# One spectral transform for keys and values and one for the weights, with partition blocks exchanged by DMA

## The reference, cut to what matters

```python
def _layernorm(x, axis=-1, eps=1e-05):
    return (x - mean) / sqrt(var + eps)

# Q = layernorm(x), K = V = ctx; B, L, D = 16, 64, 512; H = 8, topk = int(2 * log(64)) = 8
qf = jnp.fft.fft(q, axis=2)
kf = jnp.fft.fft(k, axis=2)
corr = jnp.fft.ifft(qf * jnp.conj(kf), axis=2).real
w, idx = jax.lax.top_k(corr.transpose(0, 1, 3, 2), topk)
w = jax.nn.softmax(w, axis=-1)
for i in range(topk):
    g = jnp.minimum(idx[:, :, None, :, i] + pos, L - 1)
    out = out + w[:, :, None, :, i] * jnp.take_along_axis(v, g, axis=2)
# then
x = x + tanh(g_xattn[0]) * attention
gate, up = layernorm(x) @ W_gate.T, layernorm(x) @ W_up.T      # 512 -> 1792
x = x + tanh(g_ffn[0]) * ((silu(gate) * up) @ W_down.T)
```

## Time and profile before

| | us |
|---|---|
| median of 3 runs | 226.29 (226.14 to 226.38) |
| the profiled execution, its own time | 226.31 |
| its span in the trace | 224.5 |
| PE busy, of the span | 215.6 (96%) |
| DVE busy | 149.8 (67%) |
| POOL busy | 134.2 (60%) |
| ACT busy | 98.4 (44%) |
| DMA: bytes, mean rate | 16.68 MB, 74 GB/s |

### The profile page before, as it was taken

How to read it: one execution, slowest core, us unless ns; L and a number is a source line. 1 busy time by engine, 2 the same in 40 slices (tenths; PEclk the granted TensorE clock), 3 DMA queues, 4 the chain that set the end, 5 groups by cost and what they waited for, 6 DMA issues and landing times.

```text
span 224.5 us, 6750 instructions
## 1 busy us (share of the span) xinstructions
PE 215.6 (96%) x2787; PEld 149.6 (67%) x2787; DVE 149.8 (67%) x424; ACT 98.4 (44%) x191; POOL 134.2 (60%) x148
## 2 busy tenths in 40 slices
PE   7899699799999999999999999999999999999994
PEld 2543278575395856788468965776689477967961
DVE  2799997998799777598739495576765516413321
ACT  2574146666466542744544543544414422410320
POOL 1325637989888888659774877449656292530240
PEclk9999979999999999999999999999999999999999
DMA  6899942004201122202121402202031100211001
GB/s 172 279 449 427 386 164 50 0 4 50 47 4 41 33 9 64 50 3 25 26 47 26 121 0 26 70 3 51 0 96 23 26 0 3 70 26 50 0 3 47
DMA packets 19885, 16.68 MB, mean 74 GB/s; under 512 B 15888, under 2 KB 16272, under 8 KB 19472
## 3 DMA queue, kind: packets, MB, share of 16 engines
q1 hardware_dynamic: 19856, 16.26, 25.0%
HBM read 10.49 MB, written 2.10 MB: 56 GB/s over the span
## 4 chain that ended last, share of the span: by engine, by line
PE 89%; DVE 4%; DMA 2%; POOL 1%; issue 1%; SPq 1%; ACT 0%; DVEq 0%
PE psum L825 46%; PE psum L990 22%; PE psum L808 11%; PE psum L941 4%; DMA x_sb<-x 2%; PE psum L838 1%; DVE xn L769 1%; POOL prod_lo L512 1%; DVE prod L675 1%; PE psum L877 1%; PE psum L908 1%; PE psum L889 1%; PE psum L926 1%; DVE raw_stats L644 1%; PE psum L891 1%
## 5 line engine op out<-in xcount | busy, mean ns | idle before, releaser
L825 PE MATMUL psum<-xt_hi,wg 128*128 128x128 f16 (+1 forms) x504 | 54.9, 215 | 0.0
L825 PE MATMUL psum<-xt_lo,wg 128*128 128x128 f16 (+1 forms) x504 | 54.8, 215 | 0.0
L825 PE MATMUL psum<-xt_hi,wu 128*128 128x128 f16 (+1 forms) x504 | 54.0, 213 | 0.0
L825 PE MATMUL psum<-xt_lo,wu 128*128 128x128 f16 (+1 forms) x504 | 53.9, 213 | 0.0
L825 PEld LDWEIGHTS psum<-xt_hi,wg 128*128 128x128 f16 x504 | 45.8, 99 | 5.8 <-issue 3.8
L550 POOL TENSOR_TENSOR hid_lo<-hid,hid_hi 128x512 f16<-128x512 f32 (+2 forms) x32 | 33.5, 1051 | 26.7 <-ACT hid_hi L635 26.6
L825 PEld LDWEIGHTS psum<-xt_hi,wu 128*128 128x128 f16 x504 | 44.7, 98 | 5.2 <-issue 4.7
L825 PEld LDWEIGHTS psum<-xt_lo,wg 128*128 128x128 f16 x504 | 46.1, 99 | 0.6
L825 PEld LDWEIGHTS psum<-xt_lo,wu 128*128 128x128 f16 x504 | 45.0, 98 | 0.5
L990 PE MATMUL psum<-wd,hid_hi 128*128 128x512 f16 x112 | 42.5, 379 | 0.0
L990 PE MATMUL psum<-wd,hid_lo 128*128 128x512 f16 x112 | 42.4, 379 | 0.0
(11 more groups left out here) (83 smaller groups left out, 340.3 us busy)
## 6 DMA issues: line engine op xcount, KB each, us to landing
out<-x_sb SPq DMA_DIRECT2D x8, 256.0 KB, 2.3
wg<-w_gate SPq DMA_DIRECT2D x1, 1792.0 KB, 11.2
wu<-w_up SPq DMA_DIRECT2D x1, 1792.0 KB, 14.9
wd<-w_down SPq DMA_DIRECT2D x1, 1792.0 KB, 19.0
ctx_sb<-ctx SPq DMA_DIRECT2D x1, 1024.0 KB, 21.0
x_sb<-x SPq DMA_DIRECT2D x1, 1024.0 KB, 22.8
x_sb<-x SPq DMA_DIRECT2D x2, 256.0 KB, 3.9
ctx_sb<-ctx SPq DMA_DIRECT2D x2, 256.0 KB, 4.4
```

The costliest lines, as they stand in the source:

```text
L825: last = nc.tensor.matmul(psum[:, bank, a * n:(a + 1) * n], w[:, k, m * P:(m + 1) * P], xt[:, e, k, tok], start=(k == 0 and part == 0), st ...
```

## The change

Keys and values are the same tensor, so from pair 1 on `kspec` now makes one transform of 128 different outputs: 64 of the even spectrum and 64 of the odd one (matrix "values"). `vspec` is left for pair 0 alone. `wspec` makes one transform with the 64 even and 64 odd outputs of the weights (matrix "weights") instead of two. The turned forms are no longer outputs of a matmul. Instead, ScalarE copies the two banks into `v_spec` (`vcopy`, 128 x 1024) and partitions 0 to 63 of them into `k_spec` (`kcopy`, 64 x 1024), and a new step `turn`, issued by SyncE, moves blocks of 32 partitions by DMA: `turn:p` fills the other half of `k_spec` from `v_spec` (two transfers of 32 rows of 4 KB, semaphore `k_moved`), `turn:p.1` fills `v_turned` (one of 31 rows, three of 32 rows, and the last rows of ctx from memory, semaphore `v_moved`). `prod` waits for `k_moved`, the last two `mix_prod` for `v_moved`. `mixed` has one buffer instead of two.

Both normalisations (`q_norm`, `xn`) move from VectorE to ScalarE as `Identity` with a scale and a bias per row; GpSimd makes the bias with one more operation on a column after each 1/sqrt. The loads of pair 3 move behind the second weight tensor. The warm-up groups go from 12, 4 and 9 matmuls to 12, 1 and 10. `ORDER` is a new list.

```diff
-FORWARD = ("even_kv", "even", "odd_v", "odd")
+FORWARD32 = ("even_kv", "even", "odd_v", "odd")
+FORWARD = ("query", "values", "weights")
...
+    even = np.hstack([cos(f), nyquist, -sin(f[1:])])
+    odd = np.hstack([cos(g), -sin(g)])
+    odd_v = odd.copy()
+    odd_v[-1] -= odd_v.sum(0)
...
+    return np.hstack([even, even]), np.hstack([even, odd_v]), np.hstack([even, odd]), lags, mix_plain, mix_turned
...
-        return min(p, 2) if p < 4 else 3
+        return min(p, 4)
...
-            load(ctx_sb, cv, 2, 4, ctx_loaded[2])
-            load(x_sb, xv, 2, 4, x_loaded[2])
+            load(ctx_sb, cv, 2, 3, ctx_loaded[2])
+            load(x_sb, xv, 2, 3, x_loaded[2])
             sp.dma_start(wg[:, :, :], w_gate).then_inc(gate_loaded, 16)
             sp.dma_start(wu[:, :, :], w_up).then_inc(up_loaded, 16)
+            load(ctx_sb, cv, 3, 4, ctx_loaded[3])
+            load(x_sb, xv, 3, 4, x_loaded[3])
             sp.dma_start(wd[:, :, :], w_down).then_inc(down_loaded, 16)
-            load(ctx_sb, cv, 4, PAIRS, ctx_loaded[3])
-            load(x_sb, xv, 4, PAIRS, x_loaded[3])
+            load(ctx_sb, cv, 4, PAIRS, ctx_loaded[4])
+            load(x_sb, xv, 4, PAIRS, x_loaded[4])
             for step, p, n in order:
                 e = p % 2
+                if step == "turn":
+
+                    if n == 0:
+                        sp.wait_ge(v_copied, copies(p))
+                        if p == 2:
+                            sp.wait_ge(mixed_done, 4)
+                        if p >= 2:
+                            sp.wait_ge(prod_done, 2 * p - 2)
+                        for to, first in ((64, 32), (96, 0)):
+                            sp.dma_start(k_spec[to:to + 32, e, :, :], v_spec[first:first + 32, e, :, :])\
+                              .then_inc(k_moved[e], 16)
+                    else:
+                        if p > 2:
+                            sp.wait_ge(mixed_done, 4 * p - 4)
+                        for to, first, count in ((1, 33, 31), (32, 0, 32), (64, 96, 32), (96, 64, 32)):
+                            sp.dma_start(v_turned[to:to + count, e, :, :], v_spec[first:first + count, e, :, :])\
+                              .then_inc(v_moved[e], 16)
+                        sp.dma_start(v_turned[0:1, e, :, :], last_rows[p:p + 1, :, :]).then_inc(v_moved[e], 16)
...
+                nc.gpsimd.tensor_scalar(shift[tok, n:n + 1], mean, rstd[tok, n:n + 1], -1.0, ALU.mult,
+                                        ALU.mult).then_inc(shift_done, 1)
...
+            def normalise(to, p, tok, n, normed_done):
+                nc.scalar.activation(to, x_sb[tok, p, :], ACT.Identity, bias=shift[tok, n:n + 1],
+                                     scale=rstd[tok, n:n + 1]).then_inc(normed_done, 1)
...
+                if step == "vcopy" and p > 0:
                     act.wait_ge(k_spectra, p + 1)
...
+                    nc.scalar.activation(v_spec[:, e, :, :], psum[:, k_bank(p, 0):k_bank(p, 1) + 1, :], ACT.Copy,
+                                         scale=SPEC).then_inc(v_copied, 1)
...
+                    nc.scalar.activation(k_spec[0:L, e, :, :], psum[0:L, k_bank(p, 0):k_bank(p, 1) + 1, :], ACT.Copy,
                                          scale=SPEC).then_inc(k_copied, 1)
...
                 if step == "prod":
                     dve.wait_ge(q_spectra, p + 1)
-                    dve.wait_ge(k_copied, 2 * p + n + 1)
+                    if p == 0:
+                        dve.wait_ge(k_copied, n + 1)
+                    else:
+                        dve.wait_ge(k_copied, copies(p))
+                        dve.wait_ge(k_moved[e], nth_turned(p, 2))
...
+                if step == "mix_prod" and p > 0:
+                    m, b = n // 2, n % 2
+                    dve.wait_ge(w_spectra, nth("wspec", p))
+                    if m == 0:
+                        dve.wait_ge(v_copied, copies(p))
+                    else:
+                        dve.wait_ge(v_moved[e], nth_turned(p, 5))
...
-                        last = transform(banks, "even_kv", k_hi[:, e, :], k_lo[:, e, :])
+                        last = transform(banks, "values", k_hi[:, e, :], k_lo[:, e, :])
...
-                        pe.wait_ge(k_copied, 2 * p + 2)
-                        last = transform(banks, "odd_v", k_hi[:, e, :], k_lo[:, e, :])
-                    last.then_inc(v_spectra, 1)
...
-                    else:
-                        pe.wait_ge(mixed_done, 4 * p + 2)
-                    transform([w_bank(p, n, b) for b in range(2)], ("even", "odd")[n], w_hi[:, e, :], w_lo[:, e, :])\
+                    transform([w_bank(p, 0, b) for b in range(2)], "weights", w_hi[:, e, :], w_lo[:, e, :])\
                         .then_inc(w_spectra, 1)
```

More of the change, by code:

```diff
@@ L128 @@
-prod:3 down:0.2 prod:3.1 p_hi:3 x_t:1.1 mix_prod:2 p_hi:3.1 p_lo:3 down:0.3 mix_prod:2.1 m_hi:2 p_lo:3.1
-m_hi:2.1 wspec:2.1 out:0 m_lo:2 lags:3 mix_prod:2.2 gate:1 m_hi:2.2 max:3 m_lo:2.1 mix_prod:2.3 rstd1:5 up:1
-sub:3 m_hi:2.3 m_lo:2.2 k_hi:5 match:3 exp:3 gate:1.1 m_lo:2.3 q_hi:4 sum:3 tanh:1 kspec:4 silu:1 scale:3
-tanh:1.1 stats1:6 mix:2 kcopy:4 mix:2.1 q_lo:4 kcopy:4.1 hid:1 mix:2.2 w_rows_hi:3 vspec:4 residual:2 w_t:3
-w_rows_lo:3 up:1.1 vcopy:4 vcopy:4.1 silu:1.1 rstd1:6 h_hi:1 qspec:4 h_lo:1 hid:1.1 gate:1.2 w_t:3.1 prod:4
@@ L168 @@
-down:7.3 out:7 store:7
+warm:0 stats1:0 rstd1:0 kspec:0 q_norm:0 qspec:0 kcopy:0 stats1:1 kcopy:0.1 vspec:0 prod:0 rstd1:1 k_hi:1
+prod:0.1 lags:0 vcopy:0 k_lo:1 q_norm:1 lags:0.1 warm:0.1 max:0 vcopy:0.1 sub:0 kspec:1 warm:0.2 q_hi:1
+match:0 exp:0 q_lo:1 vcopy:1 max:0.1 sum:0 kcopy:1 turn:1 scale:0 stats1:2 wt:0 qspec:1 w_hi:0 sub:0.1 rstd1:2
+gates:0 wspec:0 match:0.1 exp:0.1 turn:1.1 k_hi:2 prod:1 wspec:0.1 mix_prod:0 p_hi:1 prod:1.1 q_norm:2 mix:0
+p_lo:1 mix_prod:0.2 p_hi:1.1 sum:0.1 mix:0.1 p_lo:1.1 scales:0 scale:0.1 k_lo:2 residual:0 wt:0.1 lags:1
@@ new lines @@
+h_lo:3.2 x_t:4.1 max:6 m_hi:5.2 q_hi:7 m_lo:5 down:3.1 sub:6 m_lo:5.1 hid:3.3 exp:6 mix_prod:5.3 down:3.2
+h_hi:3.3 match:6 h_lo:3.3 m_lo:5.2 gate:4 sum:6 scale:6 down:3.3 tanh:4 m_hi:5.3 up:4 silu:4 w_rows_hi:6
+m_lo:5.3 out:3 w_t:6 turn:6.1 w_rows_lo:6 kspec:7 hid:4 mix:5 h_hi:4 q_lo:7 mix:5.1 kcopy:7 mix:5.2 gate:4.1
+w_t:6.1 residual:5 h_lo:4 vcopy:7 turn:7 up:4.1 rstd2:5 tanh:4.1 silu:4.1 xn:5 qspec:7 hid:4.1 wspec:6
+h_hi:4.1 prod:7 gate:4.2 prod:7.1 h_lo:4.1 p_hi:7 mix_prod:6 x_rows_hi:5 p_lo:7 mix_prod:6.1 x_t:5 up:4.2
```

322 lines of the change are left out of this document (165 added, 157 removed).

## The result

The changed kernel takes 256.98 us (median of 4 runs, 256.25 to 258.0), the kernel before 226.21 (4 runs, 225.94 to 226.38). The ratio is 1.135, with a 95% interval of 1.131 to 1.140. The forecast was slower, 233.0 us; the change is slower by 30.8 us and not by 7.

The account below looks back on a forecast made before the run. TensorE was taken to bound the kernel from the first gate matmul on, with a chain setting that start. First gate 45.0, the part behind it 187.2 and moved or added steps 0.8 made 233.0 us, range 227 to 238.

Parts of the forecast that it names:

- the wait at the start: Ahead of `prod:1`: first exchange queued behind all loads, landing at 32.5 us, so VectorE waits some 15 us.
- The walk from there: From the exchange's landing through pair 0 and pair 1 steps to the first gate matmul: 43.7 to 45.2 us, taken as 45.0.
- the saving on TensorE: Behind the first gate: 13 groups of six matmuls go, 9.4 us, and `kspec:2` moves ahead of it, 0.75 us.
- the price of the later exchanges: Moved or added steps, including exchanges of pairs 2 to 7: minus 1.4 to plus 5 us, taken as plus 0.8.
- dear exchanges: Rival: `turn:p.1` transfers hold the queue 4.7 us each, 5 us of waits instead of 0.8, 237.4 us or more; chance 0.13.
- the clock behind the gate: TensorE's lower clock level was expected only from 32 to 45 us; the work behind the gate got no added time.
- an exchange that passes the loads: Rival: small transfers pass the queued loads, `prod:1` starts by 17.5 us, first gate about 28.5, total 215.7 us; chance 0.10.
- The place in VectorE's row: `prod:1` stands ahead of pair 0's remaining steps on in-order VectorE, so all of pair 0 waits behind it, some 15 us.

Follow-up runs that it names:

- The run on the old order: Kernel before, with the odd transforms of ctx and of the weights left out for pairs 1 to 7, order unchanged: 220.75 us, ratio 0.975.
- the first experiment: Changed kernel with the 31-row transfer of `turn:p.1` cut into 16 and 15 rows, nothing else: 242.28 us, ratio 1.068.
- the last experiment: Kernel of 221.28 us (16 + 15 rows, `turn:1` behind `w_gate`, later transfers behind transposes) with `turn:1` ahead of the load of `w_gate`: 226.93 us, ratio 1.002.
- the one other order that was run: Changed kernel with 16 + 15 rows; pair 1's products, lags, softmax and `kspec:2` moved behind pair 0's first two `gate` and `up` groups: 242.43 us, ratio 1.073.
- 221.6: Changed kernel with 16 + 15 rows, `turn:1` behind the load of `w_gate` and later `turn:p.1` transfers behind the next transposes: 221.28 us, ratio 0.978.

## Why the prediction was right in its sign and wrong in its size

**Right: the wait at the start.** The exchange was put at 32.5 us and VectorE's wait at some 15. It ended at 33.45 after 17.3 us. The walk from there gave 45.0 for the first gate matmul, and it was 46.46, so the term is 17.5 us where 16.0 were forecast. That it is so near is in part luck, since errors of both signs stand in the walk. `max:1` came at 40.78 instead of 38.2 (37.5, and 0.7 for the clock): 0.95 of this is the later landing, and the rest the walk had not: a softmax scaling of 1.17 us where before it took 0.42, and above all `mix:0`, four float32 matmuls that took 3.68 us at half clock in the chain. `residual:0` waits for it 0.85 us, and `lags:1`, behind it on TensorE, holds `max:1` another 0.60. On the other side `kspec:2` wasn't doubled: the granted clock was 0.50 from 34 to 40 us and 1.00 from 42 on, and its six matmuls took 0.76 us. From `max:1` to its start were 4.9 us instead of 5.5.

**Right: the saving on TensorE.** 10.2 us less behind the first gate was the forecast, so 180.8 us of work. Without exchanges it is 180.0 from the first gate at 27.76 on. The run on the old order adds what the working had not considered: less work on the bound lets other engines' waits through, 2.7 us there.

**Wrong: the price of the later exchanges.** The failed step is the one that put "the price of all this" between minus 1.4 and plus 5 us and took plus 0.8, "as TensorE is 99% busy behind 28.98 with transfers of the same kind in the same places". They are not of the same kind. The prediction had the number for the 31-row transfer, 4.7 us on one engine from 431 GB/s over sixteen, beside 0.3 on all; the run with 31 rows in the exchange of `k_spec` shows it to be right (12.8 us for two, with their issue, and one DMA engine of sixteen busy in between). The rule of the Trainium skill (DMA: Bandwidth & Descriptors, Why a DMA increments its semaphore by 16 and not by 1), by which 31 rows go over one engine, is what the runs agree with: 15.1 us for cutting one transfer of seven pairs into 16 and 15. The prediction calls its rival "dear exchanges" the likely one by that rule and still gave it a chance of 0.13 and, worse, a price of 5 us in all (which makes 237.2, not the 237.4 that it wrote). So its figure for that case, 238, would have been 19 us short too. The prediction had seen that `w_t:1.1` and `x_t:1.1` stand behind such a transfer, and had not walked them: 4.7 us and SyncE's 3.6 of issuing (it had put 2) ahead of a transpose that `wspec:1` or `gate:1` waits for. These two transposes end the gaps of 6.5 and 4.7 us, and `w_t:6.1` that of 3.2. TensorE's idle time behind the first gate was put at 2.2 us and was 19.6.

**Wrong: no price for the clock behind the gate.** TensorE's work there was put at 180.8 us and took 185.4, with a mean granted clock of 0.96. Each of the three longest gaps is followed by matmuls at the lower level (0.50, 0.50 and 0.53 in the windows above). In the first experiment, with 9.9 us of idle time, the clock was 1.00 and the same work took 180.3. So these gaps cost more than their length: 9.7 us more of idle time came with 5.1 us more of work. Against the forecast, the three parts, 1.5 us later at the gate, 17.4 us of idle time and 4.6 us of work, make 23.5 of the 23.9 between 233.0 and the 256.9 of the profiled execution.

**Settled by the rest.** The chance of 0.10 for an exchange that passes the loads was given to a case that isn't there: the exchange landed at 33.3 and the last load at 32.4, and when the last experiment moved the loads, the wait moved to the next pair. The place in VectorE's row, on which the walk put weight, made no difference in the one other order that was run. The 6.6 us between 221.6 and the 215.0 without any exchange (the profiled executions) split into 2.7 us at the first gate (30.47 against 27.76) and 3.5 us of idle time behind it (5.8 against 2.3); the work is the same.

**Open.** The landing of the first exchange varies where nothing ahead of it was changed. In four profiles in which it stands behind `w_gate` with 32 rows, `w_gate` lands 9.4, 9.6, 10.9 and 12.4 us after its issue, VectorE waits 0.5, 1.4, 2.6 and 4.7 us, and the first gate starts at 28.6, 28.7, 30.5 and 32.5. It fits the queue that is worked in order, but why the load itself varies no run shows, and differences of one or two microseconds between single profiles are to be read with it in mind.
